# A transformer block on one core: GpSimd's extra work moved within the steps, and TensorE's waits moved up by one matmul

## The chip, the cores and the metric

The kernel runs on one core of one Trainium2 chip. The metric is the device time of one execution in microseconds (us), as the median of several runs. The engines of the core are TensorE (PE; its weight loads are listed apart as PEld), VectorE (DVE), ScalarE (ACT), GpSimd (POOL) and SyncE (SP), each with an instruction queue of its own that runs in order; they wait for each other through semaphores. DMAs are issued from the queues of SyncE and GpSimd.

## What is computed

Four sequences of 512 tokens with 256 features go through attention with rotary positions (32 query heads, 8 key and value heads of 64) and then through a linear layer whose input is quantised to int8 by token. Cut to what matters:

```python
x = L0_attn_x                                   # [4, 512, 256]
h = layernorm(x)
q, k, v = h @ Wq, h @ Wk, h @ Wv                # 32, 8, 8 heads of 64
q, k = apply_rope(q, pos), apply_rope(k, pos)   # k, v repeated four times
attn = softmax(where(causal, q @ k.T / 8, min))
x = x + (attn @ v).reshape(b, s, 2048) @ Wo     # [2048, 256]
h = layernorm(x)
scale = max(max(abs(h), -1), 1e-7) / 127
acc = clip(round(h / scale), -128, 127) @ weight.T      # int8, int32
x = x + float16(acc * scale * w_scale + bias)
```

## The kernel before

The work runs in 32 steps, s = 0 to 31: one step for each batch and each key and value head, that is four query heads on 512 tokens. Eight steps make a batch. The order on each engine is written out by hand: every engine has a loop over s, and the calls in it stand in the order in which the engine executes them.

**One step on TensorE.** Query tiles are taken as v = 0 to 3 (token tiles 0, 3, 2, 1). scores(s, a), a = 0 to 10, multiplies q by the high and low part of k (L704, L705) and adds the causal mask (L706), into one of three banks. VectorE takes the negative maxima (maxima, L1336), ScalarE the exponentials (exponentials, L1004), turn(s, t), t = 0 to 9, transposes a block of four heads (L719), ScalarE and VectorE split it into a high and a low part (keep_probT L1016, keep_probT_low L1325), attend(s, t) multiplies it by the values (L735, twelve matmuls). The output is normalised, turned (turn_output, L783), split and multiplied by Wo (out_product, L608); project(s + 2, j) and project_keys(s + 2) make the queries and keys of the step after the next. The calls are interleaved: TensorE's step begins with turn(s, 0), and its last calls are already scores(s + 1, 0) to (s + 1, 3). Each operation waits in its first lines for what it reads and for its bank, and the instruction that carries or follows these waits is its first matmul.

**The way of the queries.** For query pair j (two heads each) of step s + 1: ScalarE takes the projection out of PSUM (keep_raw, L943), SyncE swaps halves by DMA (L291), GpSimd rotates with three operations (rotate_second L431, rotate_first L425, rotate_sum L439), ScalarE makes the high part (keep_high, L972), GpSimd the low part (keep_low, L477), SyncE places both by four DMAs (place_queries, L327 and L328), and scores(s + 1, 0) waits for them. GpSimd's order in step s was: keep_low(s + 1, 0), rotation of pair 1 of s + 1, in even steps rotation of keys, scale_inputs (L541), **keep_low(s + 1, 1)**, then the extra work (below), keys' low part (L468), split_group_weights(s + 3) (L407, L411) and its load (L378), rotation of pair 0 of s + 2.

**The extra work of GpSimd.** In odd steps 1, 3 and 5 it is keep_wo_low(s + 1) and keep_wo_low(s + 2) (L483), the low part of two chunks of Wo, whose high part ScalarE makes (keep_wo, L929): the one of s + 1 early in ScalarE's step, the one of s + 2 after keep_probT(s, 7). From step 8 on there is the linear layer of the batch before, four token tiles. By s % 8: at 0 VectorE takes statistics; at 1 GpSimd computes the reciprocal roots (done_rstd, L513 to L525, 14 small operations) and normalises four tiles (normalise_done, L533); at 2 VectorE takes four absolute maxima (absolute_maximum) and GpSimd the scales; at 3 to 6 ScalarE, TensorE (turn_quant L758, ffn_product L772) and VectorE (keep_quant L1415, scale_product L1423) do one tile each; at 3, 5, 5 and 7 GpSimd adds bias and residual of a tile (add_bias L548, add_residual L555).

## Time and profile before

| | us |
|---|---|
| median of 3 runs (lowest, highest) | 853.73 (852.35, 855.12) |
| the profiled execution | 860.56 |
| its span | 858.8 |
| TensorE busy | 779.6 (91%) |
| VectorE busy | 635.3 (74%) |
| ScalarE busy | 628.0 (73%) |
| GpSimd busy | 572.3 (67%) |

The profile is of one execution, 6.8 us above the median of the runs. Times in the rows count from the start of the span. A busy TensorE is not one at its peak, since matmuls overlap and their ends are modelled. An idle time stands in square brackets ahead of an instruction, with the engine and line that ended it.

### The profile page before, as it was taken

To read this page: it belongs to the slowest core of one execution; us is meant where nothing else is said; L and a number is where in the kernel's file an instruction comes from. 1 tells how busy PE (TensorE), PEld (TensorE's weight loads), DVE (VectorE), ACT (ScalarE), POOL (GpSimd) and SP (SyncE) were. 2 spreads that over 40 slices of the span, in tenths; PEclk is the share of its full clock that TensorE was granted. 3 is DMA by queue.
4 is the path that set the end of the run, shared out by engine and by line. 5 is a ranking of instruction groups with operands and counts; after the bars stand their busy time and mean duration, and the time that the engine had idled before them with its cause. 6 is when DMAs were issued, how large, how long until landed. Compare 5 with 4: busy or idle time off the path is not lost.

```text
span 858.8 us, 23719 instructions
## 1 busy us (share of the span) xinstructions
PE 779.6 (91%) x8390; PEld 659.2 (77%) x8390; DVE 635.3 (74%) x1389; ACT 628.0 (73%) x1733; POOL 572.3 (67%) x524
## 2 busy tenths in 40 slices
PE   4799999999899979999999979999999979999882
PEld 3678888888787867878788867888888867888771
DVE  5657778777678757787777768777777857777884
ACT  3587878887577757778777767887777758777772
POOL 4468686868657776867767686776777687575303
PEclk9899999999899989999999999999999989999995
DMA  7255555454446434554555434454544434354300
GB/s 247 51 117 120 122 122 133 112 129 113 99 98 131 102 76 102 121 118 103 128 118 118 98 75 107 109 121 112 135 115 99 108 83 101 86 118 95 75 1 25
DMA packets 56996, 91.02 MB, mean 106 GB/s; under 512 B 12592, under 2 KB 19248, under 8 KB 56880
## 3 DMA queue, kind: packets, MB, share of 16 engines
q1 hardware_dynamic: 53808, 79.02, 40.3%
q0 software_dynamic: 3072, 10.49, 4.7%
q8 instruction: 69, 1.13, 0.6%
q14 instruction: 47, 0.39, 0.1%
HBM read 16.06 MB, written 2.10 MB: 21 GB/s over the span
## 4 chain that ended last, share of the span: by engine, by line
PE 59%; POOL 12%; DVE 7%; ACT 7%; issue 7%; DMA 5%; SPq 3%; ACTq 0%; POOLq 0%; DVEq 0%
PE x_bank L608 17%; PE t_bank L719 13%; PE o_bank L735 9%; PE s_bank L704 7%; PE s_bank L705 6%; ACT prob L1004 4%; DMA qT<-wv 3%; PE s_bank L706 3%; POOL wv L477 2%; PE t_bank L608 2%; PE ot_bank L783 2%; POOL value L533 2%; DVE probT L1325 2%; SPq L327 1%; DMA swp<-raw 1%
## 5 line engine op out<-in xcount | busy, mean ns | idle before, releaser
L1004 ACT ACTIVATE prob<-s_bank,neg_max 128x384 f32<-128x384 f32 (+3 forms) x512 | 265.8, 529 | 71.9 <-DVE neg_max L1336 71.8
L1336 DVE TENSOR_REDUCE neg_max<-s_bank 128x1 f32<-128x384 f32 (+3 forms) x352 | 217.2, 636 | 79.3 <-PE s_bank L706 76.2
L1016 ACT ACTIVATE probT<-t_bank 128x512 f16<-128x512 f32 x320 | 189.9, 600 | 64.6 <-PE t_bank L719 58.6
L1325 DVE SCALAR_TENSOR_TENSOR probT<-t_bank,probT 128x512 f16<-128x512 f32 x320 | 216.0, 683 | 24.9 <-ACT probT L1016 21.6
L719 PE MATMUL t_bank<-ident,prob 128*128 128x128 f32 x1280 | 203.1, 282 | 23.9 <-ACT prob L1004 21.6
L704 PE MATMUL s_bank<-kT,qT 128*128 128x384 f32 (+3 forms) x512 | 194.4, 381 | 10.4 <-DMA qT<-wv 7.9
L477 POOL TENSOR_TENSOR wv<-raw,wv 128x512 fp32r<-128x512 f32 x62 | 79.3, 1279 | 144.3 <-ACT wv L972 144.3
L705 PE MATMUL s_bank<-kT,qT 128*128 128x384 f32 (+3 forms) x512 | 166.0, 324 | 0.0
L719 PEld LDWEIGHTS t_bank<-ident,prob 128*128 128x128 f32 x1280 | 138.9, 143 | 34.0 <-ACT prob L1004 26.8
L735 PE MATMUL o_bank<-value,probT 128*128 128x64 f16 x3840 | 140.1, 194 | 0.0
L735 PEld LDWEIGHTS o_bank<-value,probT 128*128 128x128 f16 x3840 | 131.7, 99 | 2.6
L608 PE MATMUL x_bank<-xT,wg 128*128 128x512 f32 x468 | 128.9, 411 | 2.4 <-POOL wg L411 1.4
L608 PE MATMUL x_bank<-wo,oT 128*128 128x256 f32 x768 | 125.3, 300 | 1.4 <-DVE oT L1371 1.4
L706 PE MATMUL s_bank<-mask,ident_b 128*128 128x128 bf16 x512 | 118.7, 232 | 0.0
L704 PEld LDWEIGHTS s_bank<-kT,qT 128*128 128x128 f32 x512 | 100.9, 197 | 20.0 <-issue 11.4
L1004 ACT ACTIVATION_READ_ACCUMULATOR prob<-s_bank,neg_max 128x1 f32 x512 | 106.4, 208 | 0.0
L608 PEld LDWEIGHTS x_bank<-wo,oT 128*128 128x128 f32 x768 | 102.3, 195 | 2.2 <-DVE oT L1371 2.2
L705 PEld LDWEIGHTS s_bank<-kT,qT 128*128 128x128 f32 x512 | 99.0, 193 | 1.6
L706 PEld LDWEIGHTS s_bank<-mask,ident_b 128*128 128x128 bf16 x512 | 49.7, 97 | 61.9 <-issue 56.4
L608 PEld LDWEIGHTS x_bank<-xT,wg 128*128 128x128 f32 x468 | 83.0, 191 | 17.3 <-POOL wg L411 3.2
L439 POOL TENSOR_TENSOR raw<-raw,swp 128x512 f32<-128x512 f32 x64 | 81.9, 1280 | 10.0 <-DVE raw L1251 3.1
L1371 DVE SCALAR_TENSOR_TENSOR oT<-ot_bank,pow_rows,oT 128x256 fp32r<-128x256 f32 x128 | 61.1, 477 | 35.9 <-ACT oT L1029 35.8
(121 smaller groups left out, 1001.8 us busy)
## 6 DMA issues: line engine op xcount, KB each, us to landing
qT<-wv SPq DMA_DIRECT2D x248, 128.0 KB, 2.4
swp<-raw SPq DMA_DIRECT2D x320, 64.0 KB, 2.1
kT<-key_pair SPq DMA_DIRECT2D x128, 128.0 KB, 2.4
wg_raw<-in_w_group POOLq DMA_DIRECT2D x16, 384.0 KB, 4.6
wg_raw<-in_w_group POOLq DMA_DIRECT2D x16, 256.0 KB, 4.2
resid<-in_x SPq DMA_DIRECT2D x4, 512.0 KB, 9.4
out<-resid SPq DMA_DIRECT2D x16, 128.0 KB, 2.1
wo_stage<-in_w_out SPq DMA_DIRECT2D x4, 256.0 KB, 3.1
```

Of the source, the lines that this page charges most:

```text
L439: nc.gpsimd.tensor_tensor(raw[j][:, :], raw[j][:, :], swp[j][:, :], ALU.add).then_inc(rope_done, 1)
L477: nc.gpsimd.tensor_tensor(low, raw[j][:, :], high.bitcast(f32), ALU.subtract).then_inc(lo_kept, 1)
L608: last = nc.tensor.matmul(out_ap, left(a, k), right(b, k), start=(k == 0 and (a, b) == (HI, HI)), stop=(k == n - 1 and (a, b) == (LO, HI)))
L704: nc.tensor.matmul(bank, q, kT[s % 2][:, HI, 0:n], start=True, stop=False)
L705: nc.tensor.matmul(bank, q, kT[s % 2][:, LO, 0:n], start=False, stop=False)
L706: last = nc.tensor.matmul(bank[:, i * P:n], ident_b[:, :], mask[:, :], start=False, stop=True)
L719: last = nc.tensor.transpose(t_bank[B % TURN_BANKS][:, h * P:(h + 1) * P], prob[:, B % PROBS, h, :], ident[:, :])
L735: last = nc.tensor.matmul(o_bank[:, h * HEAD_DIM:(h + 1) * HEAD_DIM], probT[B % TURNED][:, a, h, :], value[:, c, b * Q_TILES + k, g * HEAD ...
L1004: nc.scalar.activation(prob[:, slot:slot + blocks, h, :], s_bank[G % SCORE_BANKS][:, at * n:(at + 1) * n].rearrange("p (k n) -> p k n", n= ...
L1016: nc.scalar.activation(turned_half[B % TURNED][HI], t_bank[B % TURN_BANKS][:, :], ACT.Copy, scale=PROB_SCALE).then_inc(probT_hi, 1)
L1325: nc.vector.scalar_tensor_tensor(out=turned_half[B % TURNED][LO], in0=t_bank[B % TURN_BANKS][:, :], scalar=PROB_SCALE, in1=turned_half[B % ...
L1336: nc.vector.tensor_reduce(neg_max[:, s % 2, u:u + len(heads)], s_bank[G % SCORE_BANKS][:, 0:len(heads) * n].rearrange("p (h n) -> p h n", ...
```

## The change

**GpSimd and VectorE.** Of a batch's four tiles, two are now normalised at s % 8 = 1 and two at 3; the maxima of the first two stay at 2, those of the last two go to the end of 3; scales at 2 and 4; bias and residual two tiles each at 5 and 7. On GpSimd all of the extra work (the low part of Wo included) and the scales now stand ahead of keep_low(s + 1, 1) in a step, not behind it.

**TensorE.** Each operation of the loop is cut in two: its waits (..._ready) and its matmuls. The operation in front gets the waits of the next as an argument and calls them just before its own last matmul (attend: before its last three). Where the operation in front does not exist in a step, the waits stand where they were. The waits themselves, their counts and the order of the matmuls do not change.

```diff
@@ -242,12 +242,23 @@
             tiles = tiles_at(s, 3, 1)
             return tiles[0] if tiles else None
 
-        def biased_tiles(s):
+        def tiles_of(s, phases):
 
             if not KV_HEADS <= s < STEPS:
                 return ()
-            first = batch_end(s)
-            return {3: (first,), 5: (first + 1, first + 2), 7: (first + 3,)}.get(s % KV_HEADS, ())
+            return tuple(batch_end(s) + i for i in phases.get(s % KV_HEADS, ()))
+
+        def normalised_tiles(s):
+            return tiles_of(s, {1: (0, 1), 3: (2, 3)})
+
+        def maximum_tiles(s):
+            return tiles_of(s, {2: (0, 1), 3: (2, 3)})
+
+        def scaled_tiles(s):
+            return tiles_of(s, {2: (0, 1), 4: (2, 3)})
+
+        def biased_tiles(s):
+            return tiles_of(s, {5: (0, 1), 7: (2, 3)})
...
@@ -562,17 +573,17 @@
                 rotate_keys_first(s + 2)
                 rotate_keys_second(s + 2)
                 rotate_keys_sum(s + 2)
-                scale_inputs(tiles_at(s, 2, 4))
-                keep_low(s + 1, 1)
                 if s % 2 == 1:
                     keep_wo_low(s + 1)
                     keep_wo_low(s + 2)
                 done_rstd(s)
-                for f in tiles_at(s, 1, 4):
+                for f in normalised_tiles(s):
                     normalise_done(f)
                 for f in biased_tiles(s):
                     add_bias(f)
                     add_residual(f)
+                scale_inputs(scaled_tiles(s))
+                keep_low(s + 1, 1)
                 keep_keys_low(s + 2)
                 split_group_weights(s + 3)
                 load_group_weights(s + 5)
...
 
+            def nothing():
+                pass
+
+            def split_product_then(ahead, out_ap, left, right, n):
+
+                parts = [(k, a, b) for k in range(n) for a, b in ((HI, HI), (HI, LO), (LO, HI))]
+                for k, a, b in parts:
+                    if (k, a, b) == parts[-1]:
+                        ahead()
+                    last = nc.tensor.matmul(out_ap, left(a, k), right(b, k), start=((k, a, b) == parts[0]),
+                                            stop=((k, a, b) == parts[-1]))
+                return last
+
             x_bank_free = [None]
 
             def take_x_bank(evacuated, count):
...
+                n = (i + 1) * P
                 for at, h in enumerate(heads):
                     bank, q = s_bank[G % SCORE_BANKS][:, at * n:(at + 1) * n], qT[s % 2][:, h, i * P:(i + 1) * P]
                     nc.tensor.matmul(bank, q, kT[s % 2][:, HI, 0:n], start=True, stop=False)
                     nc.tensor.matmul(bank, q, kT[s % 2][:, LO, 0:n], start=False, stop=False)
+                    if h == heads[-1]:
+                        ahead()
                     last = nc.tensor.matmul(bank[:, i * P:n], ident_b[:, :], mask[:, :], start=False, stop=True)
                 last.then_inc(scores_done, 1)
 
-            def turn(s, t):
+            def turn_ready(s, t):
                 if not inside(s):
                     return
                 B = block_no(s, t)
...
             for s in range(STEPS + 1):
+                turn(s, 0, lambda: scores_ready(s, 4))
...
+                turn_output(s, 1, lambda: turn_ready(s, 7))
+                turn(s, 7, lambda: attend_ready(s, 5))
...
+                project(s + 2, 1, lambda: turn_output_ready(s, 2))
+                turn_output(s, 2, lambda: scores_ready(s + 1, 0))
+                scores(s + 1, 0, lambda: attend_ready(s, 8))
...
@@ -1445,8 +1535,9 @@
                 maxima(s, 4)
                 maxima(s, 5)
                 keep_probT_low(s, 0)
-                for f in tiles_at(s, 2, 4)[0:2]:
-                    absolute_maximum(f)
+                if s % KV_HEADS == 2:
+                    for f in maximum_tiles(s):
+                        absolute_maximum(f)
                 keep_oT_low(s - 1, 3)
                 if s == STEPS:
                     finish_root(3, slice(LOOP_TILES, LAST_TILE))
...
                 keep_probT_low(s, 3)
                 batch_statistics(s, 1)
                 maxima(s, 9)
@@ -1478,7 +1567,7 @@
                 add_product(s, 0)
                 keep_oT_low(s, 1)
                 keep_probT_low(s, 7)
-                invert_scales(tiles_at(s, 2, 4))
+                invert_scales(scaled_tiles(s))
                 batch_aggregate(s)
                 last_statistics(s, 0)
                 add_product(s, 1)
@@ -1486,6 +1575,9 @@
                 keep_probT_low(s, 8)
                 normalise_output(s, 2)
                 keep_probT_low(s, 9)
+                if s % KV_HEADS == 3:
+                    for f in maximum_tiles(s):
+                        absolute_maximum(f)
                 last_statistics(s, 1)
                 maxima(s + 1, 0)
                 keep_oT_low(s, 2)
```

How the order of instructions moves, at three places. In these rows a name carries its buffer's number, and what stands in brackets is what the instruction waits for.

GpSimd in step 1, from the rotation of the second query pair of step 2 on; wo is the low part of Wo, wv the low part of the queries, hi_kept and wo_hi are ScalarE's. Before:

```order
L439 TENSOR_TENSOR raw1<-raw1,swp1 128x512 [waits rope_first,rope_second]
L477 TENSOR_TENSOR wv<-raw1,wv 128x512 [waits hi_kept]
L483 TENSOR_TENSOR wo<-wo_stage0,wo 128x512 [waits wo_hi]
L483 TENSOR_TENSOR wo<-ffn_rows,wo 128x512 [waits wo_hi]
L407 TENSOR_TENSOR wg0<-wg_raw0,zero 128x768 [waits proj_done,wg_loaded0]
```

After:

```order
L450 TENSOR_TENSOR raw1<-raw1,swp1 128x512 [waits rope_first,rope_second]
L494 TENSOR_TENSOR wo<-wo_stage0,wo 128x512 [waits wo_hi]
L494 TENSOR_TENSOR wo<-ffn_rows,wo 128x512 [waits wo_hi]
L488 TENSOR_TENSOR wv<-raw1,wv 128x512 [waits hi_kept]
L418 TENSOR_TENSOR wg0<-wg_raw0,zero 128x768 [waits proj_done,wg_loaded0]
```

The low part of the queries (L477, now L488) has moved behind both operations on Wo, and so behind ScalarE's wo_hi of the second.

GpSimd in step 9: the reciprocal roots (ve, rstd, tmp), the normalised tiles (value<-resid) and the low part of the queries. Before:

```order
L439 TENSOR_TENSOR raw1<-raw1,swp1 128x512 [waits rope_first,rope_second]
L477 TENSOR_TENSOR wv<-raw1,wv 128x512 [waits hi_kept]
L513 TENSOR_SCALAR ve<-mean_var 128x4 [waits aggr_done]
L515 TENSOR_SCALAR rstd<-ve 128x4 [waits norm_step]
...
L525 TENSOR_TENSOR rstd<-rstd,tmp 128x4 [waits norm_step]
L533 TENSOR_SCALAR value<-resid,mean_var,rstd 128x256 [waits norm_step] x4
L407 TENSOR_TENSOR wg0<-wg_raw0,zero 128x768 [waits proj_done,wg_loaded0]
```

After:

```order
L450 TENSOR_TENSOR raw1<-raw1,swp1 128x512 [waits rope_first,rope_second]
L524 TENSOR_SCALAR ve<-mean_var 128x4 [waits aggr_done]
L526 TENSOR_SCALAR rstd<-ve 128x4 [waits norm_step]
...
L536 TENSOR_TENSOR rstd<-rstd,tmp 128x4 [waits norm_step]
L544 TENSOR_SCALAR value<-resid,mean_var,rstd 128x256 [waits norm_step] x2
L488 TENSOR_TENSOR wv<-raw1,wv 128x512 [waits hi_kept]
L418 TENSOR_TENSOR wg0<-wg_raw0,zero 128x768 [waits proj_done,wg_loaded0]
```

The low part of the queries now comes behind the roots and two tiles; two of the four tiles are gone from this place, ahead of the split weights (wg0).

TensorE in step 12 around turn(s, 7): the end of out_product(s, 0), turn_output(s, 1) (ot_bank), turn(s, 7) (t_bank), attend(s, 5) (o_bank). Before:

```order
L608 MATMUL x_bank<-wo,oT 128x256 x5
L783 MATMUL ot_bank<-ident,o_norm 128x128 [waits oT_lo,o_normed]
L783 MATMUL ot_bank<-ident,o_norm 128x128
L719 MATMUL t_bank1<-ident,prob 128x128 [waits probT_lo,exp_done]
L719 MATMUL t_bank1<-ident,prob 128x128 x3
L735 MATMUL o_bank<-value,probT1 128x64 [waits o_normed,probT_lo]
L735 MATMUL o_bank<-value,probT1 128x64 x11
```

After:

```order
L645 MATMUL x_bank<-wo,oT 128x256 x5
L645 MATMUL x_bank<-wo,oT 128x256 [waits oT_lo,o_normed]
L855 MATMUL ot_bank<-ident,o_norm 128x128
L855 MATMUL ot_bank<-ident,o_norm 128x128 [waits probT_lo,exp_done]
L765 MATMUL t_bank1<-ident,prob 128x128 x3
L765 MATMUL t_bank1<-ident,prob 128x128 [waits o_normed,probT_lo]
L789 MATMUL o_bank<-value,probT1 128x64 x9
L789 MATMUL o_bank<-value,probT1 128x64 [waits probT_lo]
```

The waits of turn_output stand on the last matmul of out_product, those of turn(s, 7) on the second transpose of turn_output, those of attend on the last transpose of turn(s, 7).

## Rows read from the trace of the kernel before

**Rows 1.** The page: TensorE's clock in 40 slices, and one group of matmuls

```profile
PEclk9899999999899989999999999999999989999995
...
L735 PE MATMUL o_bank<-value,probT 128*128 128x64 f16 x3840 | 140.1, 194 | 0.0
```

**Rows 2.** Who waited for whom: us in total, times, longest us

```profile
DVE neg_max L1336 <- PE s_bank L706: 76.2, 90, 4.3
...
PE t_bank L719 <- ACT prob L1004: 21.6, 22, 4.1
...
ACT wv L972 <- POOL raw L439: 16.8, 5, 5.4
...
PE s_bank L704 <- DMA qT<-wv: 7.9, 11, 1.8
```

**Rows 3.** Timeline, TensorE, steps 4 and 10: start, duration, instruction, idle

```profile
149.33 0.31 PE L704 MATMUL s_bank<-kT,qT 128*128 128x128 f32 x1
...
172.62 0.31 PE L704 MATMUL s_bank<-kT,qT 128*128 128x128 f32 x1
...
294.26 0.30 PE L704 MATMUL s_bank<-kT,qT 128*128 128x128 f32 x1 [0.50 <-DMA qT<-wv]
...
307.32 1.11 PE L719 MATMUL t_bank<-ident,prob 128*128 128x128 f32 x4 [4.07 <-ACT prob L1004]
...
325.02 0.31 PE L704 MATMUL s_bank<-kT,qT 128*128 128x128 f32 x1
```

**Rows 4.** Timeline, GpSimd, step 9

```profile
287.38 1.28 POOL L477 TENSOR_TENSOR wv<-raw,wv 128x512 fp32r<-128x512 f32 x1 [4.33 <-ACT wv L972]
288.76 0.23 POOL L513 TENSOR_SCALAR ve<-mean_var 128x4 f32<-128x4 f32 x1
...
292.73 4.84 POOL L533 TENSOR_SCALAR value<-resid,mean_var,rstd 128x256 f32<-128x256 f32 x4
...
304.68 1.26 POOL L439 TENSOR_TENSOR raw<-raw,swp 128x512 f32<-128x512 f32 x1
```

**Rows 5.** Busy us in three windows: PE, PEld, DVE, ACT, POOL; clock, DMA, GB/s

```profile
307.32:313.51 6.19, 6.19 (x37) 5.51 (x38) 3.52 (x8) 3.47 (x9) 5.00 (x5) 0.51 0.33 72
404.33:407.47 3.14, 3.14 (x38) 2.97 (x38) 2.63 (x7) 2.92 (x8) 3.06 (x4) 1.00 0.19 44
221.00:228.00 7.00, 7.00 (x49) 5.96 (x50) 2.64 (x5) 2.84 (x11) 3.70 (x3) 0.51 0.55 129
```

**Rows 6.** Timeline, GpSimd, step 11

```profile
342.55 1.28 POOL L477 TENSOR_TENSOR wv<-raw,wv 128x512 fp32r<-128x512 f32 x1 [5.47 <-ACT wv L972]
343.78 0.73 POOL L548 TENSOR_TENSOR value<-value,ffn_rows 128x256 f16<-128x256 f32 x1
344.59 0.67 POOL L555 TENSOR_TENSOR resid<-resid,value 128x256 f32<-128x256 f32 x1
```

**Rows 7.** Timeline, GpSimd, step 1

```profile
97.41 1.29 POOL L477 TENSOR_TENSOR wv<-raw,wv 128x512 fp32r<-128x512 f32 x1 [4.33 <-ACT wv L972]
...
100.87 1.28 POOL L483 TENSOR_TENSOR wo<-ffn_rows,wo 128x512 fp32r<-128x512 f32 x1 [0.94 <-ACT wo L929]
```

**Rows 8.** Timeline, TensorE, the first scores of steps 2 and 7

```profile
103.59 0.30 PE L704 MATMUL s_bank<-kT,qT 128*128 128x128 f32 x1
...
220.93 0.30 PE L704 MATMUL s_bank<-kT,qT 128*128 128x128 f32 x1 [1.76 <-DMA qT<-wv]
```

**Rows 9.** Timeline, TensorE, step 14

```profile
404.78 0.51 PE L735 MATMUL o_bank<-value,probT 128*128 128x64 f16 x12
...
408.59 0.39 PE L772 MATMUL x_bank<-fwT,value 128*128 128x256 bf16 x2 [0.71 <-DVE value L1415]
...
412.65 1.56 PE L735 MATMUL o_bank<-value,probT 128*128 128x64 f16 x48
...
415.22 0.38 PE L783 MATMUL ot_bank<-ident,o_norm 128*128 128x128 f32 x2
415.63 0.63 PE L719 MATMUL t_bank<-ident,prob 128*128 128x128 f32 x4
```

184 lines of the change are left out of this document (115 added, 69 removed).

## The prediction

> **What bounds the kernel now.** I read the page first. TensorE's clock row shows full speed nearly everywhere, with dips in slices 2, 11, 15 and 33 of 40 and at the end [rows 1]. The view of who waited for whom comes next [rows 2]: TensorE's largest wait is for ScalarE's exponentials (21.6 us, 22 times, the longest 4.1), then for the DMAs that place qT (7.9 us in 11). ScalarE waited 16.8 us in 5 times, at most 5.4, for GpSimd's rotated queries, L439. TensorE is otherwise fed, so what ends late on it ends late in the kernel, and I look for the steps in which it is not fed.
>
> The timeline of TensorE [rows 3] gives a step's length as the distance from one scores(s, 0) to the next. Step 4 takes 172.62 - 149.33 = 23.3 us, step 10 takes 325.02 - 294.26 = 30.8, that is 7.5 more. In step 10 TensorE stands 4.07 us at its L719. The reason lies one step back, on GpSimd [rows 4]: in step 9 it computes the four reciprocal roots (288.76 to 292.73, 3.97 us) and the four normalised tiles (4.84 us) ahead of the next weights and the next rotation, so that L439 ends at 304.68 + 1.26 = 305.94, and ScalarE's exponentials queue behind that. The rest of the 7.5 is the clock: from 307.32 to 313.51 TensorE does at a granted 0.51 (1.2 GHz) what it does in step 14 in 3.14 us at 1.00 (2.4 GHz) [rows 5], 6.19 - 3.14 = 3.0 us lost. It fell after the standstill. 4.1 + 3.0 is the 7 us. This happens once in each of three batches (steps 10, 18, 26).
>
> **Part 1: two of four normalised tiles leave step 9.** The third and fourth go to step 11, where GpSimd sat idle 5.47 us ahead of its L477 [rows 6]; two tiles cost 4.84 / 2 = 2.4 us, so they hide there. In step 9 the roots and two tiles, 3.97 + 2.42 = 6.4 us, now stand ahead of L477 (keep_low of the second query pair), in an idle time of 4.33 us [rows 4]. GpSimd is free at 287.38 - 4.33 = 283.05, so L477 starts at 283.05 + 6.39 = 289.44, not 287.38: it is 2.06 us later. Behind it the weights and L439 come 8.8 - 2.1 = 6.7 us earlier, more than the 5.4 that ScalarE waited. So the standstill in step 10 goes, and the clock's fall with it. Gain: 7.5 x 3, less 1 because the clock's dip of the second batch does not show in the page's clock row: **-21.5 us**. What is late next in step 10 is nothing that I find; GpSimd's own margin there grows by the same 6.7.
>
> **Part 2: what L477 of step 9 releases.** It lets the queue of SyncE place qT for the next step, and the first scores wait for that. In step 9 they start 294.26 - 288.66 = 5.6 us after L477's end, and TensorE had already stood 0.50 there [rows 3, 4]. No margin is left, so 2.06 comes in full, three times: **+6.3 us**. The standstill grows to 0.50 + 2.1 = 2.6 us. One of 1.76 us at the start of step 7 [rows 8] was followed by 7 us at 0.51 [rows 5], so one of 2.6 may be too; the smaller ones of 0.5 were not. I take it for two of three at 3.0 each: **+6.0 us** (0 to 9).
>
> **Part 3: the output weights, steps 1, 3 and 5.** The new order puts both keep_wo_low ahead of keep_low as well. The first is ready at once. The second waits for ScalarE's L929, which comes late in the step: it starts at 100.87 after 0.94 us of idle, whose releaser is L929 [rows 7]. L477 started at 97.41 and had only to wait for its own copy. Now it starts at 100.87 + 1.28 = 102.15, **4.7 us later**. Before, scores(2, 0) started at 103.59 [rows 8], 4.9 us after L477's end at 98.70, without an idle bracket. How long the path must be no row tells exactly; the 4.9 to 5.6 us met here, in the second with TensorE waiting, say that the margin is between 0 and 0.8. I take 0.2, so TensorE stands 4.5 us (3.9 to 5.5). The standstill of 4.07 brought the clock down, so this one should: 3.0 more. Steps 1 and 3: 7.5 each, 15.0. Behind step 5 the time partly comes back, since the wait of 1.76 us of step 7 [rows 8] and its low clock (3.0) came from GpSimd being late, and all of GpSimd gains 3 us on a TensorE that stands: 7.5 - 4.8 = 2.7. Together **+17.7 us** (10 to 23). SyncE's queue behind the late qT holds the placing of keys and a swap; both are for later work, which moves with TensorE. ScalarE's keep_raw needs L477's result, at 103.4, and comes after that.
>
> **Part 4: bias, maxima, scales.** A bias and residual pair costs 0.73 + 0.67 = 1.4 us [rows 6]; two pairs, 2.8, fit into the 5.47 us of steps 5 and 7 of a batch, ahead of L477. The pair of step 3 leaves. In step 7 of a batch 1.4 us no longer stand behind L477, and some of the 7.9 us of qT waits [rows 2] may shrink: **-1 us** (-2 to 0). The two absolute maxima that move on VectorE go ahead of the wait for the next scores, of which VectorE has 76.2 us over the span [rows 2], so they cost nothing; were that cover gone, a tile would cost under 0.7 us. The scales take one small instruction each.
>
> **Part 5: TensorE's waits one matmul (for attend three) earlier.** Where the semaphore is there in time, a wait costs nothing now: twelve matmuls of attend take 0.51 us, and forty-eight, with three waits among them, 1.56 [rows 9]. That is (1.56 - 0.51) / 36 = 29 ns each across the waits, and (0.51 - 0.19) / 11 = 29 inside, where 0.19 is the duration of one [rows 1]. So there is nothing to gain at these. Where the semaphore comes late, the last matmul of the operation in front now stands behind the wait instead of ahead of it, and its duration is added. The place that is late in each of the 32 steps is turn(s, 7): two transposes start at 415.22, 0.11 us apart, would be over for the next at 415.44, and turn(s, 7) starts at 415.63 [rows 9]. Price 0.11 x 32 = 3.5. At ffn_product TensorE waits 0.71 us [rows 9], twelve times, with the 128-wide mask matmul of scores held: 0.06 x 12 = 0.7. At turn(s, 1) (the 22 waits of L719, three of which go) 0.06 x 19 = 1.1, at the qT waits 0.11 x 11 = 1.2. Sum 6.5, of which I let 0.5 be absorbed: **+6.0 us** (0 to 10). The held matmuls also report late: the scores in front of ffn_product free VectorE's maxima some 0.3 us later, which lies ahead of idle time on VectorE by my reading.
>
> The Trainium skill (TensorE: Matmul & The Clock Gate, Part 2, LDWEIGHTS) says that TensorE pulls weight loads ahead of matmuls in flight. By that rule a wait on the next operation's weight load could hold that load back, and moving it up would set it free. The attend rows speak against it: 29 ns with a wait between as without.
>
> **Sum.** -21.5 + 6.3 + 6.0 + 17.7 - 1.0 + 6.0 = **+13.5 us**. The sum is made against an execution of 860.56 us (span 858.8); it goes onto the median of 853.73, 6.8 lower, since the standstills are parts of the order of work and not of this one execution: 853.73 + 13.5 = **867 us**. A measurement of this kernel tells about 0.3% (2.6 us) from no change.
>
> **Rivals.**
> (a) *As summed*: 860 to 872, most likely 867. Chance 0.50.
> (b) *Faster: the moved standstills are cheap.* The clock does not fall behind the new ones, in steps 1, 3, 5, 9, 17, 25, and the late waits of part 5 are absorbed by the engines behind. Then -21.5 - 1 + 6.3 for parts 1, 2, 4; part 3 is 3.9 x 3 - 4.8 = 6.9. Sum -9.3, 844 us. It decides at the clock: with each fall kept the same sum is above zero. The rows of 4.07 and 1.76 us, both followed by the low clock [rows 3, 5, 8], speak against it. Chance 0.10.
> (c) *Faster: weight loads are set free at each boundary.* Where an operation follows another I can exclude only differences under 10 ns; 44 boundaries in 32 steps at 10 ns give -14 in place of +6: 853.73 + 7.5 - 14 = 847. Chance 0.06.
> (d) *It comes out even.* The clock stays up at steps 9, 17 and 25 (-6), the late waits cost little (-5): 856. Chance 0.16.
> (e) *Slower still: the holds travel.* The qT waits now hold the last transpose of turn_output too, ScalarE and VectorE behind it start later, and each standstill of 4.5 grows to 5.5 with two dips of the clock: 867 + 3 x 1 + 4 to 8 more, 874 to 880. Chance 0.18.
>
> **How the numbers follow.** The likeliest is 867. The range 851 to 878 leaves out (b) and (c) nearly whole and the end of (e). Faster by over 0.3% (under 851.2): (b) and (c), 0.16. Within 0.3%: most of (d), 0.13. Slower by over 0.3% (above 856.3): 0.71.
>
> **What the profile after would show.** Right: no wait of 4 us at the turn(s, 1) of steps 10, 18 and 26, and L439's wait on ScalarE gone; instead first scores of steps 2, 4 and 6 that wait 4 to 5 us for qT, with GpSimd's second keep_wo_low just ahead of L477; those of 10, 18 and 26 with 2.5 to 3; the clock low behind the longest; turn(s, 7) 0.11 us later than now after its releaser. Wrong: if scores(2, 0) waits under 2 us, part 3 is wrong, and the result is likely faster; if the spacing of matmuls across boundaries drops, (c) holds.

## The result: 866.6 us, slower by 1.25%

| | before | after |
|---|---|---|
| median (lowest, highest), us | 854.42 (852.35, 860.85), 4 runs | 866.56 (864.65, 867.40), 4 runs |
| ratio (95% interval) | 1 | 1.0125 (1.0092 to 1.0158) |
| profiled execution, span | 860.56, 858.8 | 864.65, 862.9 |
| from the first scores of step 0 to those of step 31 | 756.7 | 764.4 |

The forecast was 867. The two profiled executions are only 4.1 us apart. The steps account for 7.7 us. Against that, step 0 began at 56.12 us in the profiled execution of before and at 51.94 in that of after: before had lost some 4 us ahead of the steps, where its clock was low from 26.6 to 33.5 and that of after was not. Whole-kernel sums below therefore go by medians, and sums by step by the traces. A number is followed by "by step" where it is of the second kind.

In the code after, L704 has become L741, L706 L745, L719 L765, L735 L789, L783 L855, L477 L488, L439 L450, L483 L494, L533 L544 and L327 L338.

The page after and the view of who waited for whom (us in total, times, longest), which answer to [rows 1] and [rows 2]:

```profile
PEclk9999999998999999999999999999999999999995
...
L789 PE MATMUL o_bank<-value,probT 128*128 128x64 f16 x3840 | 145.1, 194 | 0.0
```

```profile
PE ot_bank L855 <- DMA qT<-wv: 20.9, 13, 4.0
...
PE s_bank L745 <- ACT prob L1094: 9.4, 18, 0.7
PE s_bank L745 <- DVE value L1505: 9.4, 12, 0.8
...
PE ot_bank L855 <- ACT prob L1094: 5.0, 20, 0.4
```

Two things changed hands. The 21.6 us that TensorE waited for exponentials, with 4.1 as the longest, are down to 9.4 and 5.0 with 0.7 as the longest. ScalarE's wait for L439 is gone. In exchange, the waits for the placed queries grew from 7.9 to 20.9 us, and their longest is now 4.0. The lines named are those of the operation in front: the wait now stands on a matmul of turn_output (L855) or on the mask matmul of scores (L745).

**Step 1 after**, GpSimd, SyncE's queue (SPq) and TensorE (start, duration, instruction, idle), answers to [rows 7] and [rows 8]:

```profile
89.05 1.28 POOL L494 TENSOR_TENSOR wo<-wo_stage,wo 128x512 fp32r<-128x512 f32 x1
97.20 1.28 POOL L494 TENSOR_TENSOR wo<-ffn_rows,wo 128x512 fp32r<-128x512 f32 x1 [6.87 <-ACT wo L1019]
98.43 1.31 POOL L488 TENSOR_TENSOR wv<-raw,wv 128x512 fp32r<-128x512 f32 x1
```

```profile
101.59 0.60 SPq L339 DMA_DIRECT2D qT<-wv  x1
```

```profile
104.10 0.30 PE L855 MATMUL ot_bank<-ident,o_norm 128*128 128x128 f32 x1 [4.00 <-DMA qT<-wv]
104.16 0.31 PE L741 MATMUL s_bank<-kT,qT 128*128 128x128 f32 x1
```

GpSimd stood 6.87 us waiting for ScalarE's second Wo chunk with the queries behind it. L488 ended at 99.74, TensorE stood 4.00 us, and scores(2, 0) began 4.42 us after that end. Steps 3 and 5 show the same with 3.94 and 3.99 us.

**Step 9 after**, GpSimd and TensorE, answers to [rows 4] and to the 294.26 row of [rows 3]:

```profile
299.60 2.44 POOL L544 TENSOR_SCALAR value<-resid,mean_var,rstd 128x256 f32<-128x256 f32 x2
302.02 1.26 POOL L488 TENSOR_TENSOR wv<-raw,wv 128x512 fp32r<-128x512 f32 x1
```

```profile
307.58 0.30 PE L855 MATMUL ot_bank<-ident,o_norm 128*128 128x128 f32 x1 [1.04 <-DMA qT<-wv]
307.64 0.31 PE L741 MATMUL s_bank<-kT,qT 128*128 128x128 f32 x1
```

The wait is 1.04 us, not the 2.6 that I forecast, and no low clock follows. At the first scores of steps 18 and 26 it is 1.08 and 1.75 us, and no low clock follows there either (before: 0.50, 0.72 and 0.89).

**The clock**, three windows after (busy us of PE, PEld, DVE, ACT, POOL; granted clock, DMA share, GB/s), answers to [rows 5]:

```profile
105.00:108.41 3.41, 3.41 (x34) 2.89 (x34) 1.27 (x4) 1.91 (x9) 2.88 (x3) 0.51 0.88 233
207.38:214.20 6.82, 6.10 (x44) 5.08 (x45) 1.95 (x4) 2.80 (x11) 4.50 (x4) 0.50 0.76 176
404.00:407.00 3.00, 3.00 (x45) 2.45 (x43) 1.56 (x4) 1.95 (x8) 2.81 (x3) 1.00 0.80 231
```

Behind each of the three 4 us standstills the clock is at its lower level, 1.2 GHz: from 105.0 to 108.4, from 156.2 to 159.6 and from 207.4 to 214.2. Nowhere else in the steps. In before it was low from 221.2 to 228.0, 306.5 to 313.4, 504.5 to 507.9 and 699.1 to 705.9: the second standstill of exponentials had a low stretch too, half as long as those of the other two.

Lengths of single steps, from one scores(s, 0) to the next, in us. The last three columns are experiments (below):

| step | before | after | e1 | e2 | e3 |
|---|---|---|---|---|---|
| 1 | 22.56 | 27.16 | 22.99 | 26.75 | 22.49 |
| 2 | 23.23 | 24.85 | 23.59 | 24.42 | 23.29 |
| 3 | 22.52 | 27.10 | 22.97 | 26.70 | 22.52 |
| 4 | 23.29 | 24.88 | 23.60 | 24.44 | 23.29 |
| 5 | 23.42 | 27.22 | 23.46 | 27.00 | 23.66 |
| 6 | 24.89 | 27.08 | 24.23 | 27.99 | 24.00 |
| 7 | 26.46 | 23.97 | 23.37 | 23.38 | 23.58 |
| 9 | 23.26 | 24.24 | 23.20 | 24.12 | 24.12 |
| 10 | 30.76 | 23.32 | 30.28 | 22.86 | 24.49 |
| 12 | 24.00 | 24.53 | 24.53 | 24.00 | 24.01 |
| 18 | 29.55 | 23.82 | 29.92 | 25.47 | 23.04 |
| 26 | 30.66 | 23.66 | 30.75 | 24.27 | 24.28 |

Step 12 stands for the quiet steps, those without a standstill in either kernel (12, 13, 20, 22 and others): each is some half a microsecond longer after (20 only 0.3, since it was 0.2 longer than the others in before).

### The profile page after: what moved, and what is told of

It reads as the page before. It is cut to its first block, busy times and chain, and to the rows that moved or that the text cites. A ratio compares the mean times of both kernels' runs of the same rounds, so it can differ in the third digit from the quotient of the medians.

```text
span 862.9 us, 23731 instructions
## 1 busy us (share of the span) xinstructions
PE 778.7 (90%) x8390; PEld 652.8 (76%) x8390; DVE 636.8 (74%) x1392; ACT 630.9 (73%) x1733; POOL 573.5 (66%) x527
## 3 DMA queue, kind: packets, MB, share of 16 engines
q8 instruction: 69, 1.13, 0.6%
## 4 chain that ended last, share of the span: by engine, by line
PE 56%; POOL 11%; issue 9%; DMA 7%; DVE 6%; SPq 5%; ACT 4%; ACTq 0%; POOLq 0%; DVEq 0%
PE x_bank L645 16%; PE t_bank L765 10%; PE o_bank L789 9%; PE s_bank L741 7%; PE s_bank L742 6%; DMA qT<-wv 5%; PE s_bank L745 4%; POOL wv L488 3%; PE ot_bank L855 3%; SPq L338 2%; DMA swp<-raw 2%; ACT prob L1094 1%; PE t_bank L619 1%; SPq L339 1%; POOL raw L450 1%
## 5 line engine op out<-in xcount | busy, mean ns | idle before, releaser
L765 PE MATMUL t_bank<-ident,prob 128*128 128x128 f32 x1280 | 199.0, 277 | 0.9 <-ACT prob L1094 0.5
L741 PE MATMUL s_bank<-kT,qT 128*128 128x384 f32 (+3 forms) x512 | 194.9, 382 | 0.0
L488 POOL TENSOR_TENSOR wv<-raw,wv 128x512 fp32r<-128x512 f32 x62 | 79.5, 1282 | 128.0 <-ACT wv L1062 128.0
L789 PE MATMUL o_bank<-value,probT 128*128 128x64 f16 x3840 | 145.1, 194 | 0.0
L765 PEld LDWEIGHTS t_bank<-ident,prob 128*128 128x128 f32 x1280 | 139.7, 141 | 3.4 <-ACT prob L1094 1.0
L789 PEld LDWEIGHTS o_bank<-value,probT 128*128 128x128 f16 x3840 | 133.7, 99 | 5.3
L745 PE MATMUL s_bank<-mask,ident_b 128*128 128x128 bf16 x512 | 119.2, 233 | 18.9 <-ACT prob L1094 9.4
L645 PE MATMUL x_bank<-wo,oT 128*128 128x256 f32 x768 | 129.0, 301 | 1.4 <-DVE oT L1461 1.4
L745 PEld LDWEIGHTS s_bank<-mask,ident_b 128*128 128x128 bf16 x512 | 49.9, 98 | 85.7 <-issue 41.7
L1119 ACT ACTIVATE oT<-ot_bank,pow_rows 128x256 fp32r<-128x256 f32 x128 | 60.8, 475 | 61.4 <-PE ot_bank L855 61.4
L741 PEld LDWEIGHTS s_bank<-kT,qT 128*128 128x128 f32 x512 | 103.0, 201 | 1.7 <-ACT prob L1094 0.2
L742 PEld LDWEIGHTS s_bank<-kT,qT 128*128 128x128 f32 x512 | 99.6, 195 | 1.6
L855 PE MATMUL ot_bank<-ident,o_norm 128*128 128x128 f32 x256 | 62.3, 284 | 32.7 <-DMA qT<-wv 20.9
```

The lines of the kernel that those rows point to most:

```text
L488: nc.gpsimd.tensor_tensor(low, raw[j][:, :], high.bitcast(f32), ALU.subtract).then_inc(lo_kept, 1)
L645: last = nc.tensor.matmul(out_ap, left(a, k), right(b, k), start=((k, a, b) == parts[0]), stop=((k, a, b) == parts[-1]))
L741: nc.tensor.matmul(bank, q, kT[s % 2][:, HI, 0:n], start=True, stop=False)
L742: nc.tensor.matmul(bank, q, kT[s % 2][:, LO, 0:n], start=False, stop=False)
L745: last = nc.tensor.matmul(bank[:, i * P:n], ident_b[:, :], mask[:, :], start=False, stop=True)
L765: last = nc.tensor.transpose(t_bank[B % TURN_BANKS][:, h * P:(h + 1) * P], prob[:, B % PROBS, h, :], ident[:, :])
```

## Experiments

Two questions had to be answered: what each part of the change is worth on its own, and why the moved waits, which I had put at 6 us, look like half a microsecond in each quiet step.

### e1, TensorE's waits alone

GpSimd and VectorE as before, TensorE's waits as after.

```diff
-                turn_output(s, 1)
-                turn(s, 7)
+                turn_output(s, 1, lambda: turn_ready(s, 7))
+                turn(s, 7, lambda: attend_ready(s, 5))
...
```

> TensorE's waits moved up as in the changed kernel; GpSimd and VectorE in the order and with the tables of before. Theory A (holds travel: late turn(s,7), then turn(s,8) and attend(s,7) each later): 0.5 us per step in 31 steps, with the standstills of steps 10, 18 and 26 kept: 854 + 16 = 870 us. Theory B (the price of the prediction, one held matmul at each late wait and nothing behind it): 854 + 6 = 860 us. Theory C (weight loads set free at boundaries): under 854.

Measured: 863.19 us (862.36 to 864.93), ratio 1.0097 (1.0067 to 1.0126), 7.2 us above the median of before beside it (855.96). The waits alone make the kernel slower. The figure lies between theory A and theory B. Quiet steps cost 0.53 more (step 12: 24.53 against 24.00), as theory A has it. In step 10, in which TensorE waits for something else in any case, they cost nothing that shows. Steps 6 and 7 say nothing on the price of the waits. They are together 3.8 us shorter than in the profiled execution of before (47.60 against 51.35), although GpSimd's order is the same: the wait of 1.76 us at the first scores of step 7 [rows 8] is at most 0.7 here, and no low clock follows it. In e1's view of waits:

```profile
PE ot_bank L844 <- DMA qT<-wv: 3.2, 9, 0.7
```

### e2, the moves alone

GpSimd and VectorE as after, TensorE as before.

```diff
-                scale_inputs(tiles_at(s, 2, 4))
-                keep_low(s + 1, 1)
                 if s % 2 == 1:
                     keep_wo_low(s + 1)
                     keep_wo_low(s + 2)
...
+                scale_inputs(scaled_tiles(s))
+                keep_low(s + 1, 1)
```

> GpSimd and VectorE as in the changed kernel, TensorE's waits as before. By the two traces: -21.8 for the standstills that go, +12.4 for steps 1, 3 and 5 and what follows them, +1.7 for steps 9, 17 and 25: 854 - 8 = 846 us. By the prediction's terms (-21.5 + 6.3 + 6.0 + 17.7 - 1): 854 + 7.5 = 861 us.

Measured: 853.12 us (850.15 to 856.12, 10 runs), ratio 0.9973 (0.9947 to 1.0000). Alone, the moves are worth next to nothing; neither figure on record (846 from the traces, 861 from my terms) was right. The step table says why: steps 10, 18 and 26 lose their standstill, steps 1, 3 and 5 gain one, and step 6 is longer by the low clock behind the last. The changed kernel lies 13.4 us above e2, the worth of the moved waits on top of the moves.

### e3, the second Wo chunk back behind the queries

e2 with one call put back.

```diff
                 if s % 2 == 1:
                     keep_wo_low(s + 1)
-                    keep_wo_low(s + 2)
...
                 keep_low(s + 1, 1)
+                if s % 2 == 1:
+                    keep_wo_low(s + 2)
```

> As the moves alone, but the second low part of Wo in steps 1, 3 and 5 stands behind keep_low(s+1, 1) again, the first in front. If GpSimd's wait for ScalarE's L929 is what costs in these steps, the 4 us waits for qT at the first scores of steps 2, 4 and 6 go and the kernel is about 12 us below the moves alone: 834 us. If the order of the second Wo chunk were only one of several causes there (SyncE's queue, the late rotation), under 6 us of it go: 840 or more.

Measured: 837.81 us (835.21 to 839.88), ratio 0.9805 (0.9771 to 0.9840). One call is worth 15.3 us (18.6 by step; e2's profiled execution was the longest of its ten, e3's the shortest of its four). TensorE at the first scores of step 2, in e2:

```profile
105.94 0.30 PE L715 MATMUL s_bank<-kT,qT 128*128 128x128 f32 x1 [3.99 <-DMA qT<-wv]
```

and in e3:

```profile
99.14 0.31 PE L716 MATMUL s_bank<-kT,qT 128*128 128x128 f32 x1
```

The 3.99 us bracket is gone and nothing has come in its place. Steps 1, 3 and 5 are 4.26, 4.18 and 3.34 shorter than in e2, steps 2 and 4 are 1.13 and 1.15 shorter. The second pair is the price of the clock behind each standstill. Step 6 is 4.0 shorter, behind the standstill of step 5, where the clock was low for longer; 0.9 of it is the wait for queries at its end (0.91 us against 1.77). Against before, steps 6 and 7 together are also 3.8 shorter (47.58 against 51.35). The Wo operation of 1.28 us that now stands ahead of the queries isn't shown to be the reason: e1, with it behind them as in before, takes the same 47.60, while e4, also with it behind, waits 1.72 us there and takes 49.44. The wait of 1.76 us in [rows 8] and its low clock are in good part a matter of the single execution.

### e4, two tiles out of step 9, with the order of before

The tables of after (which tiles in which step), GpSimd's order of before.

```diff
-                for f in tiles_at(s, 1, 4):
+                for f in normalised_tiles(s):
...
-                scale_inputs(tiles_at(s, 2, 4))
+                scale_inputs(scaled_tiles(s))
                 keep_low(s + 1, 1)
```

> The tables of tiles by step as in the changed kernel (two tiles normalised in step 9 of a batch, two in step 11), but all of GpSimd's extra work behind keep_low(s+1, 1) as before. Step 10's standstill was 4.1 us and 3.0 us of low clock with 8.8 us of work ahead of L439; with 2.4 less the standstill is 1.7 and the clock stays up: about 5.4 us less per batch, 854 - 16 = 838 us. If the standstill needs the roots moved too, it stays near 4 us and the kernel near 854.

Measured: 844.21 us (843.81 to 847.59), ratio 0.9881 (0.9848 to 0.9914). Part of the standstill is left, and the time lies between the two figures on record. The wait for exponentials in e4, which answers to the 21.6 row of [rows 2]:

```profile
PE t_bank L730 <- ACT prob L1015: 17.6, 23, 3.1
```

Its longest is 3.1, where it was 4.1, and step 10 takes 27.76 us, between the 30.76 of before and the 22.86 of e2. Two tiles free 2.4 us, and ScalarE waited 5.4 for L439 [rows 2]; the roots (3.97 us) have to go ahead of the queries as well for all of it.

### e5, only what fits ahead of the queries

e3 with the two tiles of step 9 behind the queries. The roots alone stay ahead: 3.97 us in an idle time of 4.33 [rows 4].

```diff
-                for f in normalised_tiles(s):
-                    normalise_done(f)
+                if s % KV_HEADS == 3:
+                    for f in normalised_tiles(s):
+                        normalise_done(f)
...
                 keep_low(s + 1, 1)
                 if s % 2 == 1:
                     keep_wo_low(s + 2)
+                if s % KV_HEADS == 1:
+                    for f in normalised_tiles(s):
+                        normalise_done(f)
```

> As e3 (second Wo part behind keep_low), and in steps 9, 17 and 25 only the roots stand ahead of keep_low, where they fit into 4.33 us of idle time; the two tiles stand behind it. If the delay of keep_low by 2 us costs 0.4 to 0.9 us in each of these steps (as the traces of the changed kernel and of e2 show): 838 - 2 = 836 us, and steps 9, 17, 25 as long as in the kernel before. If that delay costs what the prediction said, more is given back: 838 - 6 = 832.

Measured: **833.19 us** (832.47 to 834.06), ratio 0.9763 (0.9740 to 0.9786) against 854.17. It is 21.0 us under before and beats both kernels. Its page and two of its waits:

```profile
PEclk9999999999999999999999999999999999999995
```

```profile
PE t_bank L735 <- ACT prob L1020: 9.6, 20, 0.6
PE s_bank L720 <- DMA qT<-wv: 9.2, 14, 1.4
```

The figures on record were 836 and 832, and this lies between them. Over e3 it gains 4.6 us (3.5 by step), which is the price of 2.44 us of tiles ahead of the queries in steps 9, 17 and 25. The first scores of step 10, in e3:

```profile
287.87 0.30 PE L716 MATMUL s_bank<-kT,qT 128*128 128x128 f32 x1 [1.37 <-DMA qT<-wv]
```

and in e5:

```profile
286.93 0.30 PE L720 MATMUL s_bank<-kT,qT 128*128 128x128 f32 x1 [0.49 <-DMA qT<-wv]
```

The wait differs by 0.88 us, not by 2.44, and steps 9, 17 and 25 by 0.89, 1.14 and 0.74. Step 10 is another 1.05 longer in e3, where the clock was low from 289.5 to 292.9.

### e6 and e7, the moved waits on a kernel without standstills

e6 is e5 with TensorE's waits all as after. e7 is e6 with those of turn(s, 7) back:

```diff
-                turn_output(s, 1, lambda: turn_ready(s, 7))
+                turn_output(s, 1)
+                turn_ready(s, 7)
                 turn(s, 7, lambda: attend_ready(s, 5))
```

> As e5, with all of TensorE's waits moved up as in the changed kernel. In e5 few other waits are left that could absorb it. Theory A (0.5 us per step, holds travel): 15 us above e5, 851. Theory B (a held matmul at each late wait, nothing behind): 6 above e5, 842. If the waits' price of e1 (+7) holds everywhere: 843.

> As e6, but turn(s, 7) keeps its waits at its own first matmul. If the lateness of turn(s, 8) and attend(s, 7) comes from turn_output(s, 1) being held for turn(s, 7), they are in time again: steady steps under 0.15 us longer than in e5 and the kernel about 4 us above e5. If each is late by its own moved wait, only 0.1 of the 0.5 us per step goes and it is 12 us above e5.

Measured: e6 844.01 us (842.85 to 845.59), ratio 0.9890 (0.9865 to 0.9916); e7 839.33 us (838.64 to 841.90), ratio 0.9840 (0.9813 to 0.9867). The moved waits cost 10.8 us on e5. Putting back one of the some forty in each step returns 4.7, and 6.1 are left, nearer to the first figure on record (4) than to the second (12). By step e6 is 10.3 above e5: a quiet step pays 0.52, while steps 9, 10, 17, 18 and 25 pay nothing (+0.07, -0.11, +0.01, +0.01, -0.03). ScalarE's wait for turned outputs over all steps, in e5 and in e6, grows by 15 us and from 44 times to 76 (see e8 for why):

```profile
ACT oT L1045 <- PE ot_bank L799: 29.5, 44, 1.0
```

```profile
ACT oT L1124 <- PE ot_bank L860: 44.7, 76, 2.0
```

### e8, one wait alone

e5, in which only the waits of turn(s, 7) stand on the second transpose of turn_output(s, 1).

```diff
-                turn_output(s, 1)
+                turn_output(s, 1, lambda: turn_ready(s, 7))
```

> As e5, with one moved wait alone: that of turn(s, 7), now ahead of turn_output(s, 1)'s second transpose. If one held transpose costs only itself: 0.11 us per step, 3.5 us above e5. If turn_output's late result is what makes turn(s, 8) and attend(s, 7) late: 0.3 to 0.45 us per step, 9 to 14 us above e5. If TensorE gains by the early wait: below e5.

Measured: 834.57 us (833.52 to 837.05), ratio 0.9786 (0.9754 to 0.9818), 1.4 above e5. It is less than either figure that I had written down, in the whole; but a quiet step is 0.20 longer, twice the 0.11 that my prediction gave to this place. The trace shows why. ScalarE, TensorE and ScalarE again, in step 12 of e5 (it begins at 334.01):

```profile
353.25 0.20 ACT L1020 ACTIVATION_READ_ACCUMULATOR prob<-s_bank,neg_max 128x1 f32 x1
353.34 0.47 ACT L1045 ACTIVATE oT<-ot_bank,pow_rows 128x256 fp32r<-128x256 f32 x1
353.69 0.48 ACT L1020 ACTIVATE prob<-s_bank,neg_max 128x256 f32<-128x256 f32 x1
354.05 0.22 ACT L1020 ACTIVATION_READ_ACCUMULATOR prob<-s_bank,neg_max 128x1 f32 x1
354.14 0.61 ACT L1032 ACTIVATE probT<-t_bank 128x512 f16<-128x512 f32 x1
```

```profile
352.90 0.38 PE L799 MATMUL ot_bank<-ident,o_norm 128*128 128x128 f32 x2
353.31 0.63 PE L735 MATMUL t_bank<-ident,prob 128*128 128x128 f32 x4
353.77 0.86 PE L751 MATMUL o_bank<-value,probT 128*128 128x64 f16 x24
```

and in e8 (step 12 begins at 334.34):

```profile
353.57 0.20 ACT L1027 ACTIVATION_READ_ACCUMULATOR prob<-s_bank,neg_max 128x1 f32 x1
353.97 0.47 ACT L1052 ACTIVATE oT<-ot_bank,pow_rows 128x256 fp32r<-128x256 f32 x1 [0.20 <-PE ot_bank L806]
354.34 0.47 ACT L1027 ACTIVATE prob<-s_bank,neg_max 128x256 f32<-128x256 f32 x1
354.70 0.20 ACT L1027 ACTIVATION_READ_ACCUMULATOR prob<-s_bank,neg_max 128x1 f32 x1
354.79 0.60 ACT L1039 ACTIVATE probT<-t_bank 128x512 f16<-128x512 f32 x1
```

```profile
353.23 0.71 PE L806 MATMUL ot_bank<-ident,o_norm 128*128 128x128 f32 x2
353.77 0.60 PE L732 MATMUL t_bank<-ident,prob 128*128 128x128 f32 x4
```

Read against the start of the step: turn(s, 7) begins at 19.30 in e5 and at 19.43 in e8, 0.13 later, which is the held matmul. The held transpose itself begins at 19.00 in e5 and at 19.29 in e8, 0.29 later, since it now stands behind the wait. It is the instruction that tells ScalarE that the output is turned. So keep_oT (L1045, L1052) starts at 19.33 in e5 and at 19.63 in e8, after an idle time that e5 doesn't have, and the exponential and keep_probT(s, 7) behind it are 0.31 late too. The price of a moved wait has two halves: the matmul held, on TensorE, and **the late report of the operation in front**, on the engine that waits for it.

The Trainium skill (Perfetto Trace Analysis, Tensor Engine Instruction) says that a matmul's semaphore goes up only once PSUM has acknowledged its last bytes. The rows fit that: keep_oT in e8 starts 0.34 us after the start of the held transpose, whose duration is 0.30. They can't prove it, since the 0.30 is modelled.

### e9 and e10, is it three places or all of them?

e9 is e6 with three waits back at their own matmul: turn(s, 7), turn(s, 8) and attend(s, 7). e10 is e5 with only the latter two moved.

```diff
-                turn_output(s, 1, lambda: turn_ready(s, 7))
+                turn_output(s, 1)
+                turn_ready(s, 7)
...
-                attend(s, 6, lambda: turn_ready(s, 8))
+                attend(s, 6)
+                turn_ready(s, 8)
...
-                out_product(s, 1, lambda: attend_ready(s, 7))
+                out_product(s, 1)
+                attend_ready(s, 7)
```

> The kernel of e6 (GpSimd's order of e5, all of TensorE's waits moved up, 844.01 us) with three waits back at their own first matmul: those of turn(s, 7), turn(s, 8) and attend(s, 7). Theory 'three late places': these are the only places in a steady step at which the semaphore comes late and no slack swallows the held matmuls, so nearly all of the 10.8 us between e5 (833.19) and e6 goes: 833.19 + 0 to 2 = 833 to 835 us, and step 12 (24.00 us in e5, 24.51 in e6) takes 24.0 to 24.1. Theory 'spread': the some forty other moved waits each cost a little, and what is late at turn(s, 8) and attend(s, 7) is only where it comes to light; then it stays where putting back turn(s, 7) alone left it: 838 to 840 us, step 12 at 24.2.

> The kernel of e5 (833.19 us) with only two waits moved up: that of turn(s, 8) into attend(s, 6), and that of attend(s, 7) into out_product(s, 1). Theory 'three late places': attend(s, 7) then starts 0.10 to 0.15 us later in each step, as in e7, where putting all but turn(s, 7) up cost 6.1 us: + 3 to 6, 836 to 839 us, step 12 at 24.1 to 24.2. Theory 'spread': these two alone cost next to nothing, 833 to 834.5 us, step 12 at 24.0.

Measured: e9 834.74 us (834.03 to 836.51), ratio 0.9793 (0.9749 to 0.9836); e10 833.30 us (831.47 to 834.77), ratio 0.9773 (0.9734 to 0.9811). e9 is as "three late places" had it: with three of some forty waits back, 9.3 of the 10.8 us are gone, and all the others together are worth 1.5. e10 misses that theory's figure for the whole: the two waits alone cost 0.1 us (0.11 in a quiet step; step 12, 24.10, is just at the edge of its 24.1 to 24.2). So the three do their harm together. Both ran beside faster runs of before (851.09) than e5 and e6 did; by the ratios the 1.5 and the 0.1 are 2.6 and 0.9.

Quiet steps (mean of steps 12, 13, 20 and 22, by step) add up like this:

| | moved waits | us | over e5 |
|---|---|---|---|
| e5 | none | 23.92 | |
| e9 | all but three | 24.00 | +0.08 |
| e10 | turn(s, 8), attend(s, 7) | 24.03 | +0.11 |
| e8 | turn(s, 7) | 24.12 | +0.20 |
| e7 | all but turn(s, 7) | 24.13 | +0.21 |
| e6 | all | 24.43 | +0.52 |

The three kinds alone sum to 0.40; together they make 0.52. Where the 0.12 arises can be seen at turn(s, 8), which waits for the exponential of the rows above: from the start of step 12, it begins at 20.47 in e5, at 20.45 in e10, at 20.61 in e8 and at 20.80 in e6. In e10 the exponential is early enough to hide the held matmuls of attend(s, 6). With turn(s, 7) moved as well it is 0.31 late, and they are not hidden any more.

### e11 and e12, taking the late report away

Two calls of ScalarE exchanged, on e5 (e11) and on e8 (e12), so that an exponential runs while the held transpose waits.

```diff
-                keep_oT(s, 1)
                 exponentials(s, 3, 3)
+                keep_oT(s, 1)
```

> The kernel of e5 (833.19 us) with two calls of ScalarE exchanged: keep_oT(s, 1) behind exponentials(s, 3, 3), not ahead. It is the ground for e12. By the trace of e5 the exponential would start 0.35 us earlier and keep_oT 0.4 us later, out_product(s, 1) has about 0.3 us of slack for that: step 12 at 23.9 to 24.2 us (24.00 in e5), the whole 830 to 840 us.

> The kernel of e8 (e5 with only the wait of turn(s, 7) moved, onto the second transpose of turn_output(s, 1)) with the same exchange as e11. In e8 step 12 took 24.21 us, 0.21 more than in e5. Theory 'late report': the held transpose is the one that ScalarE's keep_oT waits for; it ran 0.29 us later in e8, keep_oT 0.30 us, the exponential and keep_probT(s, 7) behind it as much, and that is the price, not the 0.13 us by which turn(s, 7) itself is late. With an exponential between them keep_oT starts at 0.45 us behind its old place, after the held transpose even when that is late: e12 is then within 0.05 us of e11 in step 12 (and within 1.5 us in the whole). Theory 'own matmul': turn(s, 7) itself is 0.13 us late and all behind it on TensorE: e12 is 0.13 to 0.21 us above e11 in step 12, 2 to 5 us in the whole.

Measured: e11 832.91 us (831.27 to 835.65), ratio 0.9770 (0.9741 to 0.9798); e12 834.49 us (832.42 to 835.39), ratio 0.9784 (0.9753 to 0.9814). The exchange alone changes nothing (23.92 in a quiet step, as e5). With it the moved wait costs 0.12 in a quiet step where it had cost 0.20. Neither theory holds whole: 0.12 is the held matmul itself, just under what I had written for "own matmul", and 0.09 is the late report, which alone I had taken for everything. The rows of e12 in step 12 (it begins at 333.30) show that the report hurts nobody now:

```profile
352.19 0.70 PE L806 MATMUL ot_bank<-ident,o_norm 128*128 128x128 f32 x2
352.73 0.60 PE L732 MATMUL t_bank<-ident,prob 128*128 128x128 f32 x4
```

```profile
352.63 0.47 ACT L1027 ACTIVATE prob<-s_bank,neg_max 128x256 f32<-128x256 f32 x1
...
353.08 0.48 ACT L1052 ACTIVATE oT<-ot_bank,pow_rows 128x256 fp32r<-128x256 f32 x1
353.43 0.61 ACT L1039 ACTIVATE probT<-t_bank 128x512 f16<-128x512 f32 x1
```

turn(s, 7) still starts at 19.43, but keep_probT(s, 7) at 20.13, as in e11 (20.13), and not at 20.45 as in e8.

In the whole, e12 is 1.6 us above e11 and e8 1.4 above e5; differences of this size between medians of four runs settle nothing. The verdict rests on the quiet steps.

## Why the prediction was right in the sum and wrong in its terms

The total came out at 866.56 against 867, but the runs show four terms that were each off by 6 to 8 us in medians and cancelled. The sum was right by luck. Going from before to after one edit at a time, in medians:

| | forecast | measured | from |
|---|---|---|---|
| standstills of steps 10, 18, 26 and of step 7 go (part 1, part 4, what part 3 counted as given back) | -21.5 - 1.0 - 4.8 = -27.3 | -21.0 | before to e5 |
| two tiles ahead of the queries in steps 9, 17, 25 (part 2) | +12.3 | +4.6 | e5 to e3 |
| second Wo chunk ahead of the queries (part 3 without what comes back) | 17.7 + 4.8 = +22.5 | +15.3 | e3 to e2 |
| TensorE's waits (part 5) | +6.0 | +13.4 | e2 to after |
| sum | +13.5 | +12.3 | |

The kernels of e5 and of after ran beside other runs of before than e2 and e3 did. By the ratios instead of the medians the four are -20.2, +3.6, +14.4 and +13.0 (10.7 in sum), and by step -24.0, +3.5, +18.6 and +9.6 (7.7 in sum). So a term is known to some 4 us, and each misses its forecast in the same direction by all three measures.

**Part 1 was right in its mechanism.** The waits of 4 us at turn(s, 1) and ScalarE's wait for L439 are gone, as named. Steps 10, 18 and 26 are 7.4, 5.7 and 7.0 us shorter after, 20.2 together. I had multiplied the 7.5 of step 10 by three and taken off 1 for the one whose dip doesn't show in the clock row; step 18 alone was worth 1.8 less, and its low clock in before had lasted 3.4 us where that of the other two lasted 6.8. e4 confirms that this needs the roots ahead of the queries as well as the two tiles gone. The whole rung is smaller in medians (21.0) than by step (24.0). That fits the profiled execution of before, 6.8 us above the median: some 4 of these lie ahead of step 0, and up to 3.8 in steps 6 and 7, which e1 ran through that much faster with the same order on GpSimd.

**Part 2 failed at "no margin is left, so 2.06 comes in full".** L488's way to the first scores took 5.6 us in step 9 of before, and I took this for its length. It was not. In before, one of the four issues of SyncE took three times as long as the others. SyncE's queue in before:

```profile
289.87 1.88 SPq L327 DMA_DIRECT2D qT<-wv  x1
```

and in after:

```profile
304.49 0.60 SPq L338 DMA_DIRECT2D qT<-wv  x1
```

With 1.28 us less there, the way took 4.36 us after (302.02 + 1.26 to 307.64). So most of the delay met with a shorter way. The wait grew from 0.50 to 1.04 us, not to 2.6, no low clock followed, and in after the +6.0 for the clock was never due. The sign of the term was right and its size was nearly three times too large.

The slow issue is only one form of it. In step 25 of before and in step 9 of e5 all four issues take the usual time, and the way is long all the same (5.98 and 5.58 us), because the last of the four DMAs lands late. In e5 it is issued here, and the scores that wait for it start at 286.93:

```profile
283.20 0.60 SPq L339 DMA_DIRECT2D qT<-wv  x1
```

What goes with the long ways is a packet of 16 KB in the queue that the page lists as q8, instruction. The DMA view of before between 289.8 and 291.5, the time of the slow issue, and that of e5 between 283.3 and 284.6, the time of the last DMA, show one each:

```profile
q8 instruction: 1, 0.02, 5.6%
```

```profile
q8 instruction: 1, 0.02, 4.6%
```

The packet comes some 18.8 us into step 9 in before and in after alike. The queries were placed from 17.7 on in before, and so across it; in after they are placed from 19.9 on, behind it. In steps 9, 17 and 25 of the 11 traces in which L477 or its like starts 16.4 us into the step, the last DMA of the queries lands 4.8 to 5.9 us behind its end; in the three traces in which it starts at 18.5 or 18.6 (after, e2, e3), 4.2 to 4.9. So the delay of part 2 moved the placing out of the packet's way and somewhat over half of it (1.2 of 2.2 us) was paid back. That the packet is what makes the way long is read from when it comes; no run moved it.

**Part 3 was right in place, rows and standstill**: 4.00, 3.94 and 3.99 us measured, within the range of 3.9 to 5.5, with 4.5 taken. The way needs 4.4 us and took 4.9 in step 1 before, a margin of 0.5 where I had chosen 0.2. The clock fell as said, but the term for it was too large: behind steps 1 and 3 it was low for only 3.4 us (the first row of the windows), and e2 against e3 prices it at 1.1 us each, not 3.0; only behind step 5 is it 4.0, 0.9 of which is a longer wait for queries. I took the 3.0 from one stretch of 6.2 us [rows 5]. The time that I counted as given back in step 7 was not part 3's: e3 has no standstill and still gets it, and so does e1, with GpSimd's order of before.

**Part 4** can't be told from the rest: no run undoes it alone.

**Part 5 failed in size, by a factor of about two** (9.6 by step, 13.4 in medians, against 6.0). The step "its duration is added" was priced with the held matmul alone, 0.11 us at turn(s, 7). Measured there: 0.13 us of lateness and 0.20 us per quiet step, of which e12 gives 0.12 to the matmul and 0.09 to ScalarE's late keep_oT. I had seen that "the held matmuls also report late", but only looked for it at ffn_product and VectorE, where it lies ahead of idle time. And I had priced no wait at turn(s, 8) and attend(s, 7), since no idle bracket stood there: the slack of turn(s, 8) is about 0.2 us, which no row of waits shows, and it was used up by the late exponential. Then each of the two adds about 0.15 us (in e6, turn(s, 8) comes 0.15 and attend(s, 7) 0.16 later again). It stands in the row of attend(s, 5) and attend(s, 6) in step 14 of after, whose last three matmuls wait for that exponential:

```profile
423.81 1.01 PE L789 MATMUL o_bank<-value,probT 128*128 128x64 f16 x24
```

In e5 the same 24 take 0.86 us (its row stands with e8). At ffn_product the held mask matmul costs 0.07 us, as forecast (0.06), and its total wait goes from 8.6 us before to 9.4.

It was measured on three kernels: +7.2 us on the kernel before (e1), +10.8 on e5 (e6), +13.4 on e2. By the ratios these are 8.3, 10.8 and 13.0, and by step the last is only 9.6. That it costs on all three is clear; whether it grows where TensorE waits less isn't settled.

**The rivals.** (b), cheap standstills, falls: they cost 4 us each and the clock fell. (c), weight loads set free, falls: where the waits are met in time, 48 matmuls of attend(s, 1) to attend(s, 4) in step 14 of after take

```profile
420.26 1.56 PE L789 MATMUL o_bank<-value,probT 128*128 128x64 f16 x48
```

the same as the 1.56 us of before [rows 9], although the three waits among them have moved. The Trainium skill (TensorE: Matmul & The Clock Gate, Architectural detail, at "Engine queue depths") says that TensorE's queue can pull a weight load ahead of matmuls in flight; whether or not it does so here, moving a wait that is met in time from one matmul to another moves no start. (d) had the clock of steps 9, 17 and 25 right and the rest wrong. (e), holds that travel, describes what part 5 turned out to be, a held instruction that delays the engines behind, but at the wrong place: the standstills of 4 us did not grow (4.00 after, 3.99 in e2).

## What to carry over

Moving a wait up into the operation in front costs twice where the semaphore is late: the matmul that is held, and the report of the operation in front, which the held matmul carries; price the second at the engine that waits for that report, and look for slack that is spent by two edits at once. Extra work on a helper engine belongs ahead of a critical operation only as far as it fits the idle time there and depends on nothing late: 3.97 us in 4.33, with two tiles moved out, took away the standstills of three steps (21 us in all for e5), 2.44 us more took back 4.6, and one operation behind a late producer 15.3. And a path's length that is read off one place in the step holds for that place: here all three instances in the trace were long, and the same path was 1.2 us shorter when it began 2.2 us later.
